# Two groups of experts as one stage of 126 tiles, with the second route in parts inside it

## The reference, cut to what matters

```python
def _moe_group(x2, router_w, wg, wu, wd, top_k):
    logits = x2 @ router_w
    scores = jax.nn.softmax(logits, axis=-1)
    expert_weights, expert_indices = lax.top_k(scores, top_k)
    ...
    xs = x2[tok]                       # rows sorted by expert
    gate = lax.ragged_dot(xs, wg, group_sizes)
    up = lax.ragged_dot(xs, wu, group_sizes)
    ys = lax.ragged_dot(jax.nn.silu(gate) * up, wd, group_sizes)
    ys = ys * flat_w[order][:, None]
    return jnp.zeros_like(x2).at[tok].add(ys)
out0 = _moe_group(x2, router_w0, wg0, wu0, wd0, TOP_K)
out1 = _moe_group(x2, router_w1, wg1, wu1, wd1, TOP_K)
out = (out0 * TOP_K + out1 * TOP_K) / (TOP_K + TOP_K)
```

## Time and profile before

| | us |
|---|---|
| median of 3 runs | 2407.74 |
| lowest, highest | 2404.01, 2409.02 |
| span of the profiled execution (first to last instruction) | 2382.3 |
| PE busy in the span | 1969.4 (83%) |
| DVE busy | 1256.4 (53%) |
| ACT busy | 902.8 (38%) |
| POOL busy | 738.5 (31%) |

### The profile page before, as it was taken

How to read it: one execution, slowest core, us unless ns; L and a number is a source line. 1 busy time by engine, 2 the same in 40 slices (tenths; PEclk the granted TensorE clock), 3 DMA queues, 4 the chain that set the end, 5 groups by cost and what they waited for, 6 DMA issues and landing times. The chain is left out here.

```text
span 2382.3 us, 41693 instructions
## 1 busy us (share of the span) xinstructions
PE 1969.4 (83%) x13329; PEld 1600.1 (67%) x13329; DVE 1256.4 (53%) x4251; ACT 902.8 (38%) x2180; POOL 738.5 (31%) x927
## 2 busy tenths in 40 slices
PE   6849999986899999999669948994793973898594
PEld 5737766665888988989569935663582852565594
DVE  2542225633788888888310037774446535775423
ACT  4623222523233333333333344553442433555321
POOL 1012211101354445544111023310555734332132
PEclk9959999987999999999779969995795985899697
DMA  4232221000510111000179827426566663643294
GB/s 147 96 122 62 60 86 36 20 14 27 59 31 20 33 33 32 23 19 2 43 289 344 327 78 127 111 69 248 159 153 243 183 125 90 103 100 126 72 338 145
DMA packets 173310, 261.91 MB, mean 110 GB/s; under 512 B 23088, under 2 KB 138800, under 8 KB 169008
## 3 DMA queue, kind: packets, MB, share of 16 engines
q1 hardware_dynamic: 149584, 210.87, 28.1%
q0 software_dynamic: 16704, 45.64, 7.9%
q10 hardware_dynamic: 6816, 2.76, 1.0%
HBM read 181.19 MB, written 37.75 MB: 92 GB/s over the span
## 5 line engine op out<-in xcount | busy, mean ns | idle before, releaser
L1993 PE MATMUL heads_ps_c<-heads_band,heads_sT 128*128 128x129 f32 x3072 | 369.4, 277 | 13.8 <-DVE heads_band L2218 12.7
L1993 PEld LDWEIGHTS heads_ps_c<-heads_band,heads_sT 128*128 128x128 f32 x3072 | 355.3, 193 | 24.0 <-issue 22.1
L2156 POOL TENSOR_SCALAR heads_band<-heads_shifts,heads_taps 128x130 f32<-128x130 f32 x384 | 252.1, 670 | 242.7 <-PE heads_ps_c L1993 239.0
L508 POOL DMA_INDIRECT weights_xg<-xn_rows,token_of x197 | 189.4, 961 | 429.2 <-DVE token_of L694 168.2
L2086 ACT ACTIVATE heads_probs<-heads_mixes,heads_least 128x256 f32<-128x256 f32 x256 | 116.1, 501 | 343.5 <-DVE heads_least L2231 343.5
L2218 DVE SCALAR_TENSOR_TENSOR heads_band<-heads_shifts,heads_taps,heads_band 128x130 f32<-128x130 f32 x768 | 226.7, 350 | 18.6 <-POOL heads_band L2156 14.0
L1704 ACT ACTIVATE heads_probsT<-heads_ps_e 128x512 f32<-128x512 f32 x256 | 146.9, 598 | 134.2 <-PE heads_ps_e L1594 127.5
L1041 PE MATMUL experts_ps_g<-weights_w,experts_xT 128*128 x504 | 135.4, 393 | 0.6 <-issue 0.4
L1064 PE MATMUL experts_ps_y<-weights_w,experts_hT 128*128 (+1 forms) x486 | 133.7, 384 | 1.1 <-DVE experts_y L1126 1.1
L2231 DVE CUSTOM_DVE_ANT_0 heads_mixes<-heads_ps_c,heads_mask_add 128x256 f32<-128x256 f32 x256 | 97.9, 420 | 27.4 <-PE heads_ps_c L1993 26.8
L1098 ACT ACTIVATE experts_silu<-experts_ps_g 128x128 f32<-128x128 f32 (+1 forms) x165 | 53.0, 321 | 151.2 <-PE experts_ps_u L1046 81.3
(11 more groups left out here) (397 smaller groups left out, 4174.6 us busy)
## 6 DMA issues: line engine op xcount, KB each, us to landing
experts_w<-in_experts_dram SPq DMA_DIRECT2D x23, 2180.0 KB, 10.4
weights_w<-in_experts_dram SPq DMA_DIRECT2D x16, 1536.0 KB, 17.8
weights_w<-in_experts_dram SPq DMA_DIRECT2D x32, 768.0 KB, 5.3
heads_stackQ<-heads_pieces SPq DMA_DIRECT2D x288, 64.0 KB, 2.7
heads_stackK<-heads_pieces SPq DMA_DIRECT2D x252, 64.0 KB, 2.6
y_rows<-experts_y SPq DMA_DIRECT2D x125, 128.0 KB, 1.7
weights_w<-in_experts_dram SPq DMA_DIRECT2D x8, 1088.0 KB, 5.3
xn_rows<-xn SPq DMA_DIRECT2D x4, 2048.0 KB, 8.8
```

Source lines behind the costliest of these rows:

```text
L508: pool.indirect_dma_start(self.xg[:, u, :], None, xn_dram, bass.IndirectOffsetOnAxis(ap=tb.token_of[:, j:j + 1], axis=0)).then_inc(self.x_ ...
L1993: last = pe.matmul(out[:, qc * SEQ + k0:qc * SEQ + k1], sT[:, h % 2, kc, qc * P + dq:qc * P + dq + P], band[:, h % 2, dq, w0:w0 + k1 - k0] ...
L2156: last = pool.tensor_scalar(band[:, h % 2, dq, :], shifts[:, 0, :], taps[:, r % 2, h, dq * TAPS:dq * TAPS + 1], None, ALU.mult)
```

## The change

The stages `experts2_0`, `route2_1` and `experts2_1` become one, `two_groups_stage`, with a loop over 126 tiles. Tiles 0 to 62 are group 0, tiles 63 to 125 group 1. What it does on each engine:

- The second route is cut into 24 parts (class `SecondRoute`). VectorE does part p after `copy_out` of step p+2, ScalarE its share (Exp, digits) after step p+4, PE its share (34 matmuls) after step p+5. Its scratch space lies in xnT, and its sums go to one PSUM bank, ps_r.
- ScalarE has Silu and Exp in the same stage: one table load for Exp and one back to Silu stand among the tiles.
- SP loads experts 0 to 7 of group 1 at the start as before. The other 24 go into places that group 0 still uses, so the six transfers are placed among the output stores, after those of tiles 34, 38, 42, 46, 50 and 54.
- POOL has no late gathers until tile 71 (63+8). There it waits for `weights_ready` and until all 63 output stores of group 0 have landed, and then issues two late gathers for every third tile, 32 in all, the last after the gather of tile 116. PE waits for the loads of group 1 (`second_loaded`) before the hidden layer of tile 63.
- VectorE does the 32 `add_late` in the last 8 of its 128 steps, four in each.
- `token_of` and `weights_of` exist twice, one for each group, and `LateRows`, `FirstRows.again` and the options of `route_stage` that served the second route go.

The diff, cut to its core (`SecondRoute.scalar`, `.tensor` and most of `.vector` hold the same instructions as `route_stage`):

```diff
@@ class Resident @@
+    def load_into(self, sp, w_dram, e, slot, loaded):
+        n, W = self.together, self.W
+        rows = w_dram.rearrange("(e p) f -> p e f", p=P)
+        sp.dma_start(self.w[:, slot * W:(slot + n) * W].rearrange("p (e f) -> p e f", f=W), rows[:, e:e + n, :])\
+            .then_inc(loaded, 16)
...
@@ class SecondRoute @@
+    V_MAX, V_INDEX, V_SHIFT, V_HOT, V_SUM, V_COEF, V_SCAN, V_PLACE, V_START, V_PICK, V_SLOT, V_DIGITS, V_CHUNKS = range(13)
+    V_TOKENS = V_CHUNKS + NK // CH
+    V_ENDED, V_REDUCE, V_WEIGHTS = V_TOKENS + 1, V_TOKENS + 2, V_TOKENS + 3
+    V_PARTS = V_TOKENS + 4
...
+    def scalar(self, act, part):
+        K, CH = self.K, self.CH
+        if part == self.V_SHIFT:
+            act.wait_ge(self.shifted, 2)
+            act.activation(self.ex[:, :, :], self.ex[:, :, :], ACT.Exp).then_inc(self.exped, 1)
+            act.activation(self.ek[:, :, :], self.ek[:, :, :], ACT.Exp).then_inc(self.exped, 1)
...
@@ two_groups_stage @@
+        LATE, AFTER = 2 * TILES, 8
+        FIRST_PART, LAST_USE, TOGETHER, READY = 2, NT - E + 1, weights.together, E // 4
+
+        def passed_stores(engine, tiles):
+
+            for p in range(YB):
+                engine.wait_ge(stored[p], 16 * ((tiles + YB - 1 - p) // YB))
...
+            for j in range(first.COUNT, ALL):
+                if j >= ahead:
+                    pool.wait_ge(turned, j - ahead + 1)
+                if j == NT:
+                    pool.wait_ge(route.token_ready, 1)
+                first.gather(pool, tb.tokens[j // NT], xn_dram, j, j % NT)
+                n = (j - NT - AFTER) // 3 * 2
+                if j >= NT + AFTER and (j - NT - AFTER) % 3 == 0 and n < LATE:
+                    if n == 0:
+                        pool.wait_ge(route.weights_ready, 1)
+                        passed_stores(pool, NT)
+                    for m in (n, n + 1):
+                        pool.indirect_dma_start(late_rows[m % 2][:, m // 2, :], None, y_dram[0],
+                                                bass.IndirectOffsetOnAxis(ap=tb.slots[0][:, m:m + 1], axis=0))\
+                            .then_inc(late_in, 16)
...
+            def hidden_layer(j):
+                pe.wait_ge(xT_ready, j + 1)
+                if j >= 2:
+                    pe.wait_ge(h_ready, j - 1)
+                if j == 0:
+                    pe.wait_ge(weights.loaded, 16 * weights.transfers)
+                if j == NT:
+                    pe.wait_ge(second_loaded, 16 * (E // TOGETHER))
...
+            for step in range(ALL + 3):
+                for lag, part in enumerate((turn_rows, hidden_layer, turn_hidden, output_layer)):
+                    if 0 <= step - lag < ALL:
+                        part(step - lag)
+                route.tensor(pe, step - FIRST_PART - 3)
...
+            def add_late(n):
+                t, k = n // 2, n % 2
+                if n == 0:
+                    v.wait_ge(late_in, 16 * LATE)
+                if k:
+                    v.wait_ge(added, n)
+                v.scalar_tensor_tensor(x[:, t, :], late_rows[k][:, t, :], tb.coefs[0][:, n:n + 1], x[:, t, :],
+                                       ALU.mult, ALU.add).then_inc(added, 1)
+
+            for step in range(ALL + 2):
+                if step < ALL:
+                    multiply(step)
+                if step >= 2:
+                    copy_out(step - 2)
+                if FIRST_PART <= step < FIRST_PART + route.V_PARTS:
+                    route.vector(v, own, step - FIRST_PART)
+                n = (step - (ALL + 2 - LATE // 4)) * 4
+                if n >= 0:
+                    for m in range(n, n + 4):
+                        add_late(m)
...
+            for e in range(0, READY, TOGETHER):
+                weights.load_into(sp, w_second, e, slots[1] + e, second_loaded)
+            e = READY
+            for j in range(ALL):
+                sp.wait_ge(y_copied, j + 1)
+                sp.dma_start(y_dram[j // NT][j % NT * P:(j % NT + 1) * P, :], y[:, j % YB, :]).then_inc(stored[j % YB], 16)
+                if e < E and j + 1 >= LAST_USE + e - READY + TOGETHER - 1:
+                    weights.load_into(sp, w_second, e, slots[1] + e, second_loaded)
+                    e += TOGETHER
+            passed_stores(sp, ALL)
...
@@ build @@
-            resident_experts_stage(core, "experts2_0", NT, 32, [P], resident, 8, tb, first, xn_dram, y_dram,
-                                   ident, ones, prefetch=lambda sp: resident.load(sp, i["experts2_1"], 0, 8, 0))
-            rows_0 = (xn, xnT[:, :, :].rearrange("p c n -> p (c n)").rearrange("p (t d) -> p t d", d=D))
-            late = LateRows(x, rows_0, tb.slot_of, tb.coef, y_dram[0:NT * P, :])
+            room = xnT[:, :, :].rearrange("p c n -> p (c n)")
+            late_rows = (xn, room.rearrange("p (t d) -> p t d", d=D))
+            two_groups_stage(core, "experts2", NT, 32, resident, i["experts2_1"], (8, 0),
+                             lambda s, bank: SecondRoute(s, logits[:, :, 32:64], NT, tb, ones, bank, room, 0.5),
+                             tb, first, xn_dram, (y_dram[0:NT * P, :], y_second[0:NT * P, :]), x, late_rows, ident, ones)
             tb.use(1)
-            first.again(NT)
-            route_stage(core, "route2_1", logits[:, :, 32:64], 32, 2, NT, tb, ones, None, xn_dram, first, factor=0.5,
-                        prefetch=lambda sp: resident.load(sp, i["experts2_1"], 8, 32, 8), late=late)
-            resident_experts_stage(core, "experts2_1", NT, 32, [P], resident, 0, tb, first, xn_dram, y_second,
-                                   ident, ones, late=late)
```

More of the change, by code:

```diff
@@ L474, in __init__ @@
         self.iota16, self.zeros16 = core.keep("iota16", [P, P], BF16), core.keep("zeros16", [P, P], BF16)
-        self.token_of = core.keep("token_of", [P, most_tiles], U32)
-        self.weights_of = core.keep("weights_of", [P, most_tiles], U32)
+        self.tokens = [core.keep(f"token_of{n}", [P, most_tiles], U32) for n in range(2)]
+        self.weights = [core.keep(f"weights_of{n}", [P, most_tiles], U32) for n in range(2)]
         self.slots = [core.keep(f"slot_of{n}", [P, TILES * 2], U32) for n in range(2)]
@@ L494, in __init__, with gather, route_stage @@
         self.x_in = [s.sem(f"x_in{u}") for u in range(ahead)]
-        self.past = [0] * ahead
-    def again(self, NT):
-        for j in range(NT):
-            self.past[j % self.ahead] += 1
     def wait(self, engine, j):
         u = j % self.ahead
-        engine.wait_ge(self.x_in[u], 16 * (self.past[u] + j // self.ahead + 1))
-    def gather(self, pool, tb, xn_dram, j):
-        u = j % self.ahead
+        engine.wait_ge(self.x_in[u], 16 * (j // self.ahead + 1))
+    def gather(self, pool, token_of, xn_dram, j, tile=None):
+        u, n = j % self.ahead, j if tile is None else tile
         pool.indirect_dma_start(self.xg[:, u, :], None, xn_dram,
-                                bass.IndirectOffsetOnAxis(ap=tb.token_of[:, j:j + 1], axis=0)).then_inc(self.x_in[u], 16)
-def route_stage(core, name, lg, E, K, NT, tb, ones, xn, xn_dram, first, bias=None, capacity=None, factor=1.0,
-                prefetch=None, late=None):
+                                bass.IndirectOffsetOnAxis(ap=token_of[:, n:n + 1], axis=0)).then_inc(self.x_in[u], 16)
+def route_stage(core, name, lg, E, K, NT, tb, ones, xn, xn_dram, first, bias=None, capacity=None, factor=1.0):
     NK, CH = TILES * K, 4
@@ L795, in _ @@
                     pool.wait_ge(turned, j - ahead + 1)
-                first.gather(pool, tb, xn_dram, j)
+                first.gather(pool, tb.token_of, xn_dram, j)
         @block.tensor
@@ L970, in load @@
             self.transfers += 1
[L973 to L986 removed]
+    def load_into(self, sp, w_dram, e, slot, loaded):
[3 more added lines that the diff above has]
+            .then_inc(loaded, 16)
 def resident_experts_stage(core, name, NT, E, chunks, weights, slot, tb, first, xn_dram, y_dram, ident, ones,
[L990 removed]
+                           prefetch=None):
     F, NF = sum(chunks), len(chunks)
@@ L1008, in resident_experts_stage @@
         h_ready, h_turned, hT_ready = s.sem("h_ready"), s.sem("h_turned"), s.sem("hT_ready")
-        y_ready, y_copied, added, late_in = (s.sem(n) for n in ("y_ready", "y_copied", "added", "late_in"))
+        y_ready, y_copied = s.sem("y_ready"), s.sem("y_copied")
         block = s.block()
@@ L1016, in _ @@
                     pool.wait_ge(turned, j - ahead + 1)
-                first.gather(pool, tb, xn_dram, j)
-                if late is not None and j % 3 == 0 and late.EARLY <= j // 3 + late.EARLY - 2 < 2 * TILES:
-                    late.gather(pool, j // 3 + late.EARLY - 2, j // 3 + late.EARLY - 1, late_in)
+                first.gather(pool, tb.token_of, xn_dram, j)
         @block.tensor
@@ L1141, in _ @@
                     copy_out(step - 2)
-                if late is not None and step < late.EARLY:
-                    add_late(step)
```

(2 more changed lines are left out.)

287 lines of the change are left out of this document (255 added, 32 removed).

## The result

| | median us | lowest, highest | runs |
|---|---|---|---|
| before | 2407.85 | 2399.43, 2409.02 | 6 |
| changed | 2421.44 | 2415.13, 2423.15 | 6 |

The ratio is 1.0061, 95% interval 1.0047 to 1.0075: slower by some 14.7 us. The forecast was 2402, range 2386 to 2417: the change was to gain 5.5 us and lost 14.7, and the time lies above the range. The changed kernel run again later gave 1.0073 (1.0056 to 1.0090).

The account below looks back on a forecast made before the run. The prediction took PE to bound both expert stages, with a 43.6 us hole between them. Removing 57.5 us, less five terms (9 + 10 + 20 + 3 + 10 = 52), gains 5.5 us: 2402.2 us, range 2386 to 2417.

Parts of the forecast that it names:

- stage without stalls: Merged expert stage: the first group's 105.7 us plus 63 tiles of 1.62 us, 207.8 us if nothing stalls.
- route parts: First group's tiles: uneven route parts, table loads and PE's 34 matmuls stall the stream 9 us, bounds 4 and 16.
- six loads: First group's last tiles: weight loads among the stores delay gathers and stores, 10 us, bounds 2 and 22.
- POOL in the second group: Second group: POOL's gathers, 1.25 us from start to start, make PE wait 20 us, bounds 15 and 26.
- left-over tiles: Group 1 tiles whose 128 slots name one row: slow gathers, with no POOL lead left, cost 3 us, bounds 0 and 8.
- adds: Last eight steps: VectorE's 32 adds take 20.5 us where about 10 are needed; 10 us exposed, bounds 8 and 12.
- old sum: Kernel before, first hidden layer to last copy: 105.7 + 43.6 + 116.0 = 265.3 us.
- The base: Whole program: the median lies 25.4 us above the profiled span and nothing outside changes, so span 2376.8 becomes 2402.2.
- Rival C: Second group: POOL does not bound; gathers come faster than 1.25 us, 20 us go, 2382; chance 0.06 together with another rival.
- The clock should hold: Second group: granted clock stays up, as it was 1.00 at 8.63 of 10 us busy; stops are 1.4 us.
- rival S: In e8's expectation: TensorE waits for a gather's completion that is reported late, so nothing changes, 2415 to 2421.
- Rival B: Tiles 41 to 63: loads jam the stores, costing 22 us instead of 10; slower, 2417; chance 0.20.

Follow-up runs that it names:

- e3: The changed kernel without the second group's route in the first group's tiles, using the first group's tables; ratio 1.0018, 12 us less than the changed kernel.
- e2: The changed kernel without the six weight loads among the first group's last 22 tiles; ratio 0.9984, 20 us less than the changed kernel.
- e1: The changed kernel without the 32 late gathers, the adds kept; ratio 0.9890, 42 us less than the changed kernel.
- e0: The kernel before, unedited, profiled again; span 2396.0, that execution's own time 2397.84, median 2400.52 us, ratio 1.0009.
- e9: The changed kernel with one late gather every fifth tile, 11 in all, the other 21 left out and the adds kept; ratio 0.9963.
- e4: The changed kernel with each late gather replaced by a GpSimd tensor operation on the same buffer row, same waits for stores; ratio 0.9945.
- f1: The changed kernel with the 32 late gathers replaced by 32 plain 128 KB transfers issued by SyncE; ratio 0.9882.
- f2: The changed kernel with late gathers of 256 bytes a row instead of 1 KB; ratio 1.0081.
- e5: The changed kernel with late gathers reading xn_rows by the first group's token table instead of y_rows by slot_of; ratio 1.0073.
- f6: The changed kernel again, unedited, beside runs of the kernel before; 2418.09 us, ratio 1.0073.
- e8: The changed kernel with the second group's 63 expert numbers fixed in the program instead of loaded into a register at each tile; ratio 1.0073.
- f5: The changed kernel with a ring of 4 row buffers instead of 8 in the layer's two groups; ratio 1.0039.

## Why the prediction was wrong

Floor and terms, as the prediction put them, and as measured:

| step | predicted (bounds) | profile of the changed kernel | run without it |
|---|---|---|---|
| stage without stalls | 207.8 | 207.8 | |
| route parts | 9 (4 to 16) | 13.3 | 12 (e3) |
| six loads | 10 (2 to 22) | 18.9 | 20 (e2) |
| POOL in the second group | 20 (15 to 26) | 14.8 + 34.8 | 42 (e1) |
| left-over tiles | 3 (0 to 8) | 0 | |
| adds | 10 (8 to 12) | 8.7 | |
| sum | 259.8 | 298.3 | |
| old sum | 265.3 | 274.7 (e0) | |

*The base.* "The median of the runs shown lies 25.4 above the span, and nothing outside changes" was wrong in its reading: by the later profiles 1.8 us lie around the span, and the other 23.6 were the difference between an unusual execution and a usual one. Of the 13.7 us that the second profile shows of it, 10.0 lay in the second group, in the very stretch being changed. The rows were thus the best case. This error alone made the forecast too low in gain, not too high: with 274.7 for 265.3 the same terms give 15 us.

*POOL in the second group* is the step that failed, and it alone turns the sign: 20 us (15 to 26) were forecast, and without the late gathers 42 go (e1). The step said that GpSimd's starts, 1.25 us apart, set the pace, that PE waits for rows once the lead of eight is spent, and that three tiles then take 6.25 us. What the runs showed in its place: three tiles take 7.5 us; GpSimd's starts are 1.25 apart four times of five, and the fifth waits for PE, which the prediction had the other way round; the delay comes at once, with a lead of eight as of four; and five tiles slow down (e9) where GpSimd's starts would leave it idle. Only e4, without the late transfers, runs by the mechanism forecast, and it costs 13 us. That indirect transfers on GpSimd's queue cause the rest is shown (e1, f1, f2, e5); by what means is not. In the first profile tiles 72 to 112 are 13.3 periods of 2.6 us too much, 34.8, and the hole adds 14.8, which was in no term; in f6's profile the two are 30.9 and 14.6. Both sums lie above e1's 42, which compares medians. The hole is not the lost lead alone: e4 waits 7.5 us for the same stores and has no hole. Rival C's title, that POOL does not bound, came true without its gain: the gathers came no faster, and the tiles got slower. "The clock should hold": the granted clock was 0.68 over the hole, 0.50 from 1845.5 us on, after PE had been busy 0.84 us in 4.5; over the tiles of the loads it was 0.87.

The beginning of the hole in the changed kernel's timeline. A turn ends at 1838.15, ScalarE's copy of it begins at 1840.20; the next turn ends at 1839.78, its copy begins at 1850.87:

```profile
1837.77 0.38 PE L1351 MATMUL experts_ps_x<-ident,weights_xg 128*128 128x128 f32 x2
...
1839.40 0.38 PE L1351 MATMUL experts_ps_x<-ident,weights_xg 128*128 128x128 f32 x2
...
1840.20 0.37 ACT L1399 COPY experts_xT<-experts_ps_x 128x256 f32<-128x256 f32 x1 [2.34 <-PE experts_ps_x L1351]
...
1840.72 1.12 PE L1367 MATMUL experts_ps_g<-weights_w,experts_xT 128*128 x4 [0.93 <-ACT experts_xT L1399]
...
1850.87 0.37 ACT L1399 COPY experts_xT<-experts_ps_x 128x256 f32<-128x256 f32 x1 [5.40 <-DMA heads_stackQ<-heads_max_rows]
```

In settled tiles a copy begins 0.04 us behind its turn. (The releaser named in the last row is of another stage; it only says that the profile found none.) And no row was missing. The transfers of 1832 to 1836 us, by queue:

```profile
DMA packets 289, 0.27 MB, mean 68 GB/s; under 512 B 32, under 2 KB 288, under 8 KB 288
## 3 DMA queue, kind: packets, MB, share of 16 engines
q1 hardware_dynamic: 288, 0.26, 19.7%
q14 instruction: 1, 0.01, 0.7%
```

GpSimd's queue, q0, has no packet there, though gathers up to tile 71's were issued by 1828: their rows had landed. A second witness is GpSimd, whose tile gather waits for nothing but a turn. The turn of tile 72 is recorded from 1847.00 to 1847.63; ScalarE's copy of it and the gather that waits for it:

```profile
1854.73 0.39 ACT L1399 COPY experts_xT<-experts_ps_x 128x256 f32<-128x256 f32 x1
1854.77 0.95 POOL L503 DMA_INDIRECT weights_xg<-xn_rows,token_of  x1 [2.72 <-DMA heads_stackQ<-heads_max_rows]
```

Both start some 7 us behind the recorded end, as if the turn had ended only then; f6 has the same pair at 1853.93 and 1853.97. So it is not ScalarE that is slow: PE's result reaches both engines late, or PE's records show its work earlier than it was done. Which of the two, and why indirect transfers bring it about, stays open, as does how one execution of the kernel before ran 60 us of them at full rate. PE's register load is ruled out as the cause (e8), rival S of that run is not. The Trainium skill (DMA: Bandwidth & Descriptors, Latency and other measured facts) gives contention of the software queue's descriptor rings for SBUF's ports as a best guess at something near this, that DMA engines 7 and 15 are usually slower. No run here shows it; f2, with few bytes and as many rows, doesn't speak against it.

*Loads.* Rival B's place and bound (22) were right: "if over 16, B". Measured 19. The prediction worked out a surplus of 15 us and then took only 10 of it, since "only gathers and stores may run late"; but late stores stop PE, as rival B said. With 19 for 10 the forecast would have read 2411.

*Route.* 13 us, in its bounds. The fitting chunks took 1.86 us a tile, not 1.63, and the last two heavy parts 2.8 each. ScalarE's two table loads in the changed kernel's timeline, the same view as the earlier trace rows:

```profile
1704.45 0.27 ACT L1412 COPY experts_hT<-experts_ps_h 128x128 f32<-128x128 f32 x1 [0.81 <-PE experts_ps_h L1376]
1704.73 1.28 ACT L1259 ACT_TABLE_LOAD   x1
1706.02 0.63 ACT L1259 ACTIVATE xnT<-xnT 128x512 f32<-128x512 f32 x1
...
1707.05 1.28 ACT L1406 ACT_TABLE_LOAD   x1
```

The Trainium skill (ScalarE: Activation LUTs, What ACT_TABLE_LOAD costs) names a drain of 1380 ns beside the load. The trace disagrees: the load begins 0.01 us behind the copy, the Exp 0.01 us behind the load, and 1.28 us was the whole price of a switch.

*Left-over tiles* cost nothing: from tile 112 on tiles take 1.63 us again. *Adds:* 8.7 for 10, right.

## What to carry to other kernels

Compare the profiled execution's own time with the median before taking durations from it: a gap that isn't around the span is time that some stage usually loses, and it may be the stage you change. In this kernel an indirect transfer by GpSimd had a price in the stream that it ran beside: 42 us for 32, or 1.3 us each, whether it brought 1 KB or 256 bytes a row. So count such transfers and not their bytes, measure one where they run beside the stream and not alone, and let a queue of SyncE carry what needs no indices. When transfers must fit into a stretch that is already at 0.70 of the engines, take the surplus as stall in full: here 15 us of surplus became 19.

## What the hardware showed that was not expected

- 32 indirect transfers of 4 MB in all cost 42 us beside the tiles; 32 plain ones of the same bytes cost nothing measurable (f1 against e1, 0.9882 and 0.9890).
- The same kernel's second group ran in 116.0 us in one execution and 126.1 in another, with a mean granted clock of 0.95 both times.
- Four buffers of lead did no worse than eight (f5 1.0039, changed 1.0061 and 1.0073).
